# An adaLN block on 8 cores: the fp8 weight staging stores straight from its load buffer, without the GpSimd copy between

## What is computed

```python
mod = (silu(c) @ wmod).reshape(8, 6, 1, -1)          # sa, ca, ga, sb, cb, gb
ga = sign(ga) * max(|ga|, 0.25);  gb = sign(gb) * max(|gb|, 0.25)
h = layernorm(x) * (1 + ca) + sa
x = x + ga * local_attention(h)                       # 16 heads, 4 kv heads, window 512
h = layernorm(x) * (1 + cb) + sb
gate = silu((h @ fp8(gate_w)) * gate_scale)           # gate_w, up_w: 2048 x 6144
up   = (h @ fp8(up_w)) * up_scale
x = x + gb * (((gate * up) @ fp8(down_w)) * down_scale)   # down_w: 6144 x 2048
```

## Time and profile before

| | us |
|---|---|
| median of the 2 timed runs | 4030.35 (4027.75 to 4032.96) |
| the profiled execution | 4023.1 |
| its span on core 6, the slowest | 4021.5 |
| spans of the eight cores | 4000.4 to 4021.5 |
| mean granted clock of TensorE, all cores | 0.895 to 0.901 of full speed |

### The profile page before, as it was taken

How to read it: one execution, slowest core, us unless ns; L and a number is a source line. 1 busy time by engine, 2 the same in 40 slices (tenths; PEclk the granted TensorE clock), 3 DMA queues, 4 the chain that set the end, 5 groups by cost and what they waited for, 6 DMA issues and landing times.

```text
span 4021.5 us, 48786 instructions; the slowest of 8 cores (4000.4 to 4021.5 us)
## 1 busy us (share of the span) xinstructions
PE 3271.7 (81%) x16778; PEld 1540.9 (38%) x16778; DVE 806.1 (20%) x1682; ACT 773.6 (19%) x1329; POOL 475.8 (12%) x664
## 2 busy tenths in 40 slices
PE   2344539996666668978999969999889999699999
PEld 0011214444444334434444434444334444344444
DVE  3200101005555552021110131110211101311101
ACT  2100500115555553122010020110021000210100
POOL 1011000014444444200000100000000000000000
PEclk9566569998888888988999979999989999799999
DMA  8898291369999999721223422223322233222232
GB/s 171 175 152 148 47 115 16 37 53 100 92 95 99 100 106 116 94 74 55 76 79 100 123 87 74 79 87 107 121 69 79 74 101 114 94 75 78 74 123 98
DMA packets 475306, 377.76 MB, mean 94 GB/s; under 512 B 384928, under 2 KB 387680, under 8 KB 470720
## 3 DMA queue, kind: packets, MB, share of 16 engines
q0 software_dynamic: 372928, 181.67, 39.0%
q1 hardware_dynamic: 102144, 192.97, 15.0%
HBM read 505.40 MB, written 62.96 MB: 141 GB/s over the span
## 4 chain that ended last, share of the span: by engine, by line
PE 75%; DMA 8%; issue 6%; DVE 5%; ACT 3%; another core or an unknown queue 2%; DVEq 0%; ACTq 0%; POOL 0%; POOLq 0%; SPq 0%
PE PSf L865 17%; PE PSf L927 17%; PE PSf L875 16%; PE PSf L698 6%; PE PSf L545 5%; DMA wmodb<-wmod 5%; PE PSf L598 2%; PE PSf L581 2%; DMA s_x<-x 2%; PE PSf L612 2%; PE PSf L501 2%; PE PSf L585 1%; PE PSf L518 1%; ACT s_p L646 1%
## 5 line engine op out<-in xcount | busy, mean ns | idle before, releaser
L865 PE MATMUL PSf<-h,g 128*128 128x512 bf16 x3072 | 703.4, 383 | 4.5 <-ACT h L837 4.5
L875 PE MATMUL PSf<-h,u8w 128*128 128x512 bf16 x3072 | 694.4, 379 | 0.0
L927 PE MATMUL PSf<-fuse,d 128*128 128x512 bf16 x3072 | 676.2, 380 | 8.1 <-DVE fuse L892 8.1
L865 PEld LDWEIGHTS PSf<-h,g 128*128 128x128 fp8e4 x3072 | 302.4, 99 | 374.0 <-issue 17.7
L875 PEld LDWEIGHTS PSf<-h,u8w 128*128 128x128 fp8e4 x3072 | 300.6, 98 | 362.5
L927 PEld LDWEIGHTS PSf<-fuse,d 128*128 128x128 fp8e4 x3072 | 298.7, 98 | 360.8 <-issue 14.4
L892 DVE SCALAR_TENSOR_TENSOR fuse<-PSf,gsus,sy 128x512 bf16<-128x512 f32 x192 | 144.1, 751 | 1254.2 <-ACT sy L887 1254.2
L887 ACT ACTIVATE sy<-PSf,gsus 128x512 bf16<-128x512 f32 x192 | 132.0, 687 | 1164.2 <-PE PSf L875 1164.2
L382 PE MATMUL PSf<-wmodb,csi 128*1 128x512 bf16 x384 | 158.8, 578 | 227.6 <-DMA wmodb<-wmod 213.1
L581 PE MATMUL PSf<-k_fm,q_fm 128*128 128x512 bf16 x256 | 116.1, 454 | 206.6 <-ACT s_p L646 200.7
L968 POOL DMA_DIRECT2D s_xe<-x x64 | 34.5, 539 | 1866.0 <-DVE fuse L892 1653.4
(11 more groups left out here) (106 smaller groups left out, 2254.7 us busy)
## 6 DMA issues: line engine op xcount, KB each, us to landing
wmodb<-wmod POOLq DMA_DIRECT2D x64, 768.0 KB, 15.8
g<-g_scr SPq DMA_DIRECT2D x192, 256.0 KB, 2.6
u8w<-u_scr SPq DMA_DIRECT2D x192, 256.0 KB, 2.9
d<-d_scr SPq DMA_DIRECT2D x64, 768.0 KB, 4.8
s_x<-x SPq DMA_DIRECT2D x16, 1024.0 KB, 13.1
s_u<-x SPq DMA_DIRECT2D x16, 1024.0 KB, 6.2
s_xe<-x POOLq DMA_DIRECT2D x64, 256.0 KB, 3.5
y<-x3p POOLq DMA_DIRECT2D x64, 256.0 KB, 4.5
```

The costliest lines, as they stand in the source:

```text
L865: ev("pe", lambda e, par=par, kc=kc: e.matmul(bankf(0 + par), g8[:, par, :].rearrange("p (c n) -> p c n", c=16)[:, kc, :].bitcast(F8), h2[ ...
L875: ev("pe", lambda e, par=par, kc=kc: e.matmul(bankf(2 + par), u8w[:, par, :].rearrange("p (c n) -> p c n", c=16)[:, kc, :].bitcast(F8), h2 ...
L927: ev("pe", lambda e, par=par, m=m_, dbk=dbk: e.matmul(bankf(dbk), d8[:, par, :].rearrange("p (a n) -> p a n", a=NM)[:, m, :].bitcast(F8), ...
```

## The change

The third of `preu8` and the copy are gone, with the counter's bookkeeping. The store reads `pre8` directly, with both sides typed uint32. Because the store now reads the buffer that a later load overwrites, load `si` waits for store `si-3`.

```diff
     pre8 = sb("pre8", [128, 3, 2048], F8, off=O_TOP)
-    preu8 = sb("preu8", [128, 3, 2048], U8, off=OFFS["x3p"])
...
             par = si % 3
             lp = si % 2
+            w = [st_done[si - 3]] if si - 3 in st_done else []
             ev("gp", lambda e, psrc=psrc, par=par: e.dma_start(
                 pre8[:, par, :].rearrange("p (c n) -> p c n", n=128), psrc),
-               sc=dPre2[lp], waits=[(c_lau, lau_done.get(si - 3, 0))])
+               sc=dPre2[lp], waits=w)
...
-            w = [ld_done[sj]]
-            if sj - 3 in st_done:
-                w.append(st_done[sj - 3])
-            ev("gp", lambda e, par=par: e.tensor_copy(
-                preu8[:, par, :].bitcast(U32), pre8[:, par, :].bitcast(U32)),
-               inc=c_lau, waits=w)
-            lau_done[sj] = c_lau.n
             ev("gp", lambda e, dst=dst, par=par: e.dma_start(
-                dst, preu8[:, par, :]),
-               sc=dScr2[lp], waits=[(c_lau, c_lau.n)])
+                dst.bitcast(U32), pre8[:, par, :].bitcast(U32)),
+               sc=dScr2[lp], waits=[ld_done[sj]])
             st_done[sj] = (dScr2[lp], dScr2[lp].n)
```

More of the change, by code:

```diff
@@ L724, in build @@
                 d_scr[dc][:, 2048 * sub:2048 * (sub + 1)]))
-    lau_done = {}
     st_done = {}
```

## The result

The changed kernel is slower: 1.0765 times the time of before (95% interval 1.074 to 1.079). Against the 4030 us of before that is 4339 us, 308 us more; its profiled execution took 4364.1 us. The forecast was 4187 us, in a range of 4070 to 4310. The direction and the mechanism were right, but the delay was forecast at about half its size, and the time lies above the range. (Some executions of both kernels fell into the slower state of the machine; they are left out of every ratio here.)

A forecast was written before the change was run, and what follows sets the result against it. DMA bounds the staging, which has 159 us of slack before the gate products. 143 steps of 7.6 us, plus 8.9 for the last and 20 for Wo, delay them 164 us: 4023.1 + 164 = 4187 us, range 4070 to 4310.

The forecast's parts named there:

- Slack: Staging on core 6 could end as late as 1824.5 us, 159 us later, before the first gate product was delayed.
- A store is served behind the load issued before it: In the staging's DMA queue: a store lands after the load issued before it, so the new wait empties the queue.
- rival 1: Staging loop: steps stay under 6.5 us, so the slack hides them; about 4010 us, chance 0.08.
- lone load: Staging load with no other load in flight: 6.2 us to landing, taken from the q-weight load as nearest row.
- the 20 us set aside for Wo: Wo's loads share the DMA with the staging: 14 loads at 1.3 us, about 20 us added to its end.
- The choice between the bounds: Staging step: 7.6 us taken between sums of 7.3 and 8.0, with outer bounds of 6.6 and 8.9.
- The second working: Staging step: 5.40 us of queue work plus 1.8 to first packet, 0.4 to landing and 0.4 restart, 8.0 us.
- The outer bound of 8.9 us: Staging step if the store starts only after the load: 6.2 + 2.3 + 0.4 us.
- Attention: Attention beside the staging: removing the copy gains 0 to 24 us (0.6%), worth nothing while the staging decides the end.
- The slack holds it: Staging loop: steps under 6.5 us never reach PE; about 4010 us, chance 0.08.
- The long step: Staging step above 8.5 us, from store completion following the load's or slow 8-bit writes; 8.9 gives 4373 us, chance 0.07.
- The signs: Expected trace: no copy, loads 7 to 8.5 us apart landing after 6 to 7, staging past 1900 us, PE idle.

The follow-up runs named there:

- The pair of 36 and 72 slow steps: Kernel before, with load `si` also waiting for store `si-3`, only in the first 36 steps (1.001 of before) or the first 72 (1.0261).

## Why the prediction was right and where it failed

**Slack: right.** It was 159 us on core 6. The pair of 36 and 72 slow steps shows both sides of it, and the 322 us of idle PE show what is behind it.

**A store is served behind the load issued before it: right**, and it carried the case as the prediction said. In the changed kernel it lands 1.15 + 6.9 - 7.3 = 0.75 us after that load. Issuing the store ahead of the next load takes the loss away, in one queue and, with the stores on SP, across two. The Trainium skill states in "DMA: Bandwidth & Descriptors", section "Two DMAs through the same engine are not ordered", that within one queue of a DMA engine the descriptors start in order. The landings within POOL's queue agree with it, but the same 0.7 us behind the load from SP's queue shows that it is not needed for them. So the lane of its own in which a store would land after 2.3 us, which rival 1 asked for, was not there when SP issued the stores.

**The sum of a step: the term that failed is the lone load.** The prediction added 6.2 + 0.7 + 0.4 = 7.3 us and took 7.6. The measured terms for a gate step are:

| term | predicted | measured |
|---|---|---|
| load, issue to landing | 6.2 | 7.3 |
| store, behind the load | 0.7 | 0.75 |
| restart | 0.4 | 0.6 |
| sum | 7.3, taken as 7.6 | 8.65; mean of all steps 8.73 |

The restart is from the timeline of a down step: a store is issued at 2036.07, stores land 6.5 us later there in the median, and the next load starts at 2043.20. The load's 1.1 us has three parts. A gate load is 0.6 us slower than the q-weight load with writes of the same size (6.8), 0.1 comes with its narrower writes (6.9, alone), and 0.4 is there once a store is issued 1.15 us behind each load (7.3). That the store's packets slow the load's last ones is likely but not shown. The nearest row was a good choice for the lone down load and a poor one for two thirds of the steps; the trace gave a hint of it, since in the kernel before the loads of `gw` and `uw` landed after 10.5 and 10.2 us in the median and those of `dw` after 9.4.

On core 6 of the execution after, the books close: (8.74 - 7.6) x 143 = 163 us more from the steps, less the 20 us set aside for Wo, which these steps contain already, less 9.5 us for a staging that began earlier (864.7 instead of 874.2), plus the forecast's 164 give 298 us to the nearest us, and the first gate product stands at 2128.2, which is 298 us after 1830.1.

**The choice between the bounds: wrong.** The second working, 5.40 us of work plus the exposed fixed times, gave 8.0 and was nearer. I went towards the smaller one because "a core that reads less also disturbs its neighbours less", which no row showed. The outer bound of 8.9 us held, but the range ended at 8.45. Its low end has a slip as well, which did no harm: by the prediction's own sum a step of 6.9 us gives about 4087 us and not 4070.

**Attention: right in kind.** The prediction bounded the gain at 24 us and set it at nothing for the total. It is 11 us: attention takes 640.8 us without copies and 649.4 to 652.9 with 121 to 131 of them beside it, and 645.2 to 648.5 in the experiment with the copy and the wait, where slower steps put fewer copies beside attention. With six and four buffers and with the order turned about as many steps run beside attention as before, without the copies, and attention takes 640.6 to 642.0 us, so it is the copies and not the DMA issues. The Trainium skill, "SBUF — State Buffer", section "Who interferes with whom", says that a DVE instruction in a two-port mode and a GpSimd instruction use one pair of ports, and that the one that issues first holds it for its whole duration while the other is blocked. The trace agrees in kind, with up to 1045 ns for an instruction of 254, but this instruction takes up to 916 ns in the changed kernel too, where POOL only issues DMAs. Nor do its long cases alone make the 11 us: on the slowest core it has a mean of 309 ns with six buffers and 304 with the copy and the wait, and attention takes 640.8 and 646.6 us. How the copies cost attention its time is therefore open. With four buffers and with the order turned these 11 us, 0.27%, are most of the gain of 0.3 to 0.4%.

**The rivals.** "The slack holds it" fell. The estimate by the formula of the Trainium skill, "DMA: Bandwidth & Descriptors", section "Anatomy of one DMA — SWDGE (gpsimd) path" (4.4 us for the load), was 2 us or more too low for rows of 512 B: alone they take 6.4 to 7.2 us. For the store it was near (2.6, measured 2.3 to 2.4). The long step was the case that came, at 8.73 us, but neither of the reasons given for it was the main one.

**The signs.** No copy, the staging past 1900 us, PE idle in front of the gate products, a chain through the scratch and an unchanged rest all came as listed. The size did not: loads start 8.7 us apart and land after 7.3, just outside the 7 to 8.5 and the 6 to 7 given.

**Open.** Whether 24 KB between rows costs the half us was not tried by itself. Why a store from another queue still lands behind the load is not shown. And six buffers gain less than four or than the turned order (0.999 against 0.997 and 0.996), with Wo 223 to 232 us long on the eight cores instead of 223 to 226 in the turned order; on core 0 PE waited twice for a Wo load there, 3.7 us in all, which doesn't explain the whole.

## What to carry to other kernels

A copy that looks idle can be what frees a buffer before its store has landed: when it goes, ask for which landing the next load then waits, and which load was issued before that transfer, from whichever queue. If a buffer is freed by a store, issue that store before the next load, or have one buffer more than the loads in flight and the store need; here either turned 7.7% lost into 0.3 to 0.4% gained. And when a lone transfer has to be priced from a neighbour, match the distance of its source rows too, and end the range at the outer bound of the sum.

## What the runs showed of the hardware

- Loads of 2048 rows of 512 B with a cast, alone in the queue: 6.3 to 6.4 us for the down weights (rows 8 KB apart), 6.8 to 7.2 us for gate and up (24 KB apart; the distance was not varied by itself). 16-bit instead of 8-bit writes make 0.1 us for gate and down and 0.4 for up.
- A 256 KB store lands after 2.3 to 2.4 us alone. Beside loads it lands 0.7 us behind the load issued before it, within POOL's queue and from SP's: after 8.4 us in the loop of before, 5.8 with the order turned, 5.9 from SP.
- From the landing of a DMA to the start of the one that waits for it on POOL: 0.6 us.
- 121 to 131 GpSimd copies of 0.62 us beside attention cost it 11 us, 0.09 us for each copy.
